# The first normalisation of a two-layer recurrent/attention network: its 128-row transposes made as pairs of 64-row transposes

## What is computed

```python
x = L0_attn_x                      # (4, 1024, 256)
xn = _layernorm(x, axis=-1)
s = _L0_attn_ref(xn, ...)          # begins with h = _layernorm(xn, ln_g, ln_b), then Q, K, V = h @ W.T
g = _silu(_L0_ffn_ref(xn, ...))    # begins with logits = xn @ gate_w.T (16 experts)
x = x + s * g
xn = _layernorm(x, axis=-1)
s = _L1_attn_ref(xn, ...)          # 16 heads of 64, causal softmax
g = _silu(_L1_ffn_ref(xn, ...))    # 8 experts, top 2
x = x + s * g
```

## Time and profile before

| | us |
|---|---|
| Median of three runs | 2710.64 |
| The three runs | 2716.63, 2710.22, 2710.64 |
| The profiled execution | 2716.68 |
| Its span | 2714.9 |
| First normalisation, first to last TensorE work | 19.14 to 64.49 |
| First TensorE work of the next stage | 67.65 |

### The profile page before, as it was taken

How to read it: one execution, slowest core, us unless ns; L and a number is a source line. 1 busy time by engine, 2 the same in 40 slices (tenths; PEclk the granted TensorE clock), 3 DMA queues, 4 the chain that set the end, 5 groups by cost and what they waited for, 6 DMA issues and landing times. The chain is left out here.

```text
span 2714.9 us, 45734 instructions
## 1 busy us (share of the span) xinstructions
PE 2490.7 (92%) x14584; PEld 1728.2 (64%) x14585; DVE 1288.0 (47%) x3160; ACT 1132.6 (42%) x2593; POOL 536.7 (20%) x485
## 2 busy tenths in 40 slices
PE   6999996999992689999999999999999998999993
PEld 6445553555551556666666666666666667999993
DVE  5454542211224546556566566565655653333334
ACT  3122121111112446666666666666666664222222
POOL 3000002444423133233111111111111110111113
PEclk8999998999995589999999999999999999999997
DMA  5001012876434333222211112111221124667796
GB/s 183 31 31 46 15 46 94 255 215 179 116 70 119 125 117 101 78 85 82 57 31 46 46 44 56 39 39 46 62 55 46 54 66 156 240 235 240 243 332 225
DMA packets 144829, 295.30 MB, mean 109 GB/s; under 512 B 16784, under 2 KB 102560, under 8 KB 134400
## 3 DMA queue, kind: packets, MB, share of 16 engines
q1 hardware_dynamic: 123824, 251.62, 29.0%
q0 software_dynamic: 20944, 42.94, 6.2%
HBM read 193.83 MB, written 67.12 MB: 96 GB/s over the span
## 5 line engine op out<-in xcount | busy, mean ns | idle before, releaser
L1364 DVE CUSTOM_DVE_ANT_0 at_p<-at_ps,atk_mask 128x640 f32<-128x640 f32 (+7 forms) x512 | 375.7, 753 | 262.7 <-PE at_ps L1228 147.9
L1282 ACT ACTIVATE at_pT<-at_ps 128x512 f32<-128x512 f32 (+1 forms) x640 | 327.1, 554 | 214.8 <-PE at_ps L1228 213.3
L1275 ACT ACTIVATE at_p<-at_p,at_nmax 128x640 f32<-128x640 f32 (+7 forms) x512 | 391.5, 768 | 58.1 <-DVE at_nmax L1364 55.8
L1307 POOL TENSOR_TENSOR at_qkT<-at_raw,at_swapped 128x1024 f32<-128x1024 f32 x64 | 150.8, 2356 | 1033.7 <-DVE at_swapped L1379 1033.7
L1228 PEld LDWEIGHTS at_ps<-atk_ident,at_p 128*128 128x128 f32 x2304 | 255.6, 141 | 142.6 <-issue 127.6
L1394 DVE SCALAR_TENSOR_TENSOR late_y<-at_ps,at_inv,late_y 128x256 f32<-128x256 f32 x512 | 215.1, 477 | 224.5 <-PE at_ps L1249 205.8
L1228 PE MATMUL at_ps<-atk_ident,at_p 128*128 128x128 f32 x2304 | 316.1, 278 | 5.3 <-ACT at_pT L1282 3.3
L1218 PE MATMUL at_ps<-at_qkT 64*128 64x512 f32 (+3 forms) x1536 | 292.5, 499 | 6.9 <-POOL at_qkT L1307 3.8
L1239 PE MATMUL at_ps<-at_pT,at_v 128*64 128x256 f32 (+1 forms) x2560 | 277.2, 363 | 0.0
L1200 PE MATMUL at_ps<-atk_h,atk_w 128*128 128x512 f32 x512 | 242.7, 597 | 15.5 <-SPq L1074 15.5
L1239 PEld LDWEIGHTS at_ps<-at_pT,at_v 128*64 128x64 f32 x2560 | 172.2, 136 | 99.4 <-issue 21.2
(11 more groups left out here) (214 smaller groups left out, 3300.0 us busy)
## 6 DMA issues: line engine op xcount, KB each, us to landing
moe_w<-in_w_w SPq DMA_DIRECT2D x53, 1028.0 KB, 4.5
at_swapped<-at_raw SPq DMA_DIRECT2D x256, 128.0 KB
late_w<-in_w_w SPq DMA_DIRECT2D x18, 1028.0 KB, 4.4
atk_w<-in_w_qkv SPq DMA_DIRECT2D x32, 384.0 KB
slot_in<-ex_zero SPq DMA_DIRECT2D x9, 1032.0 KB
xn_n<-n_stage SPq DMA_DIRECT2D x8, 1024.0 KB, 4.6
ex_wg<-in_w_eg SPq DMA_DIRECT2D x16, 512.0 KB
ex_wu<-in_w_eu SPq DMA_DIRECT2D x16, 512.0 KB
```

The lines of the kernel that those rows point to most:

```text
L1275: act.activation(buf, buf, ACT.Exp, bias=nmax[:, unit:unit + 1], scale=-1.0, accum_out=rsum[:, unit:unit + 1]).then_inc(exp_done, 1)
L1282: act.activation(dst, ring[RING_BANK[part][ev]][:, 0:(i1 - i0) * P].rearrange("p (k c) -> p k c", c=P), ACT.Copy).then_inc(t_read, 1)
L1307: pool.tensor_tensor(out=qkT[x][:, :].rearrange("p (m t) -> p m t", m=2)[:, :, half * CH:(half + 1) * CH], in0=raw[half][:, :].rearrange(" ...
L1364: dve.tensor_tensor_reduce(out=p[unit % LAG][:, 0:(n[0] + 1) * P], in0=scores(*n), in1=mask[:, T - (n[0] + 1) * P:T], scale=-1.0, scalar=3 ...
```

## The change

Only the call with `first` true is changed. Each 128 x 128 transpose becomes two: the upper 64 rows of the block and the lower 64 rows of it, each with the 64 x 64 corner of the identity as moving data. The two are issued one behind the other, in different row halves of TensorE, and they write 64 columns each to two different banks. Three pairs of banks (0 and 1, 2 and 3, 4 and 5) are used in turn by the half batches of `turn_stage` and `turn_scaled`. A half batch now fills a pair of banks with both halves of the channels (`c`), so ScalarE's evictions of a half batch both wait until its 16 half transposes are done. An eviction reads 256 columns of each of the two banks and puts them in order in `xnT` or `hT`. TensorE waits, before a half batch, for the evictions of the half batch three before it, in a common order of `stage` and `scaled`. The logits and the order of the three steps of a batch stay as they were.

```diff
+        def half_pair(b, kind, half):
+
+            at = (4 * b + 2 * kind + half) % 3 * 2 * CH
+            return s.all_banks[:, at:at + 2 * CH].rearrange("p (r c i x) -> p c r i x", r=2, c=KC, x=DH)
...
+                def turn_halves(b, kind, src, signal):
+
+                    for half in range(2):
+                        event = 4 * b + 2 * kind + half - 3
+                        if event >= 0:
+                            pe.wait_ge((stage_read, scaled_read)[event % 4 // 2], 4 * (event // 4) + 2 * (event % 2) + 2 + ONE)
+                        for c in range(KC):
+                            for i in range(4):
+                                at = (half * 4 + i) * C + c * P
+                                for r in range(2):
+                                    rows = slice(r * DH, (r + 1) * DH)
+                                    last = pe.transpose(half_pair(b, kind, half)[:, c, r, i, :], src[rows, at:at + P], ident[rows, rows])
+                            last.then_inc(signal, 1)
+
                 def turn_stage(b):
+                    if first:
+                        return turn_halves(b, 0, stage[b % 2], stage_ps)
...
                 def turn_scaled(b):
                     pe.wait_ge(scaled_made, b + 1 + ONE)
+                    if first:
+                        return turn_halves(b, 1, scaled[b % 2], scaled_ps)
...
                 def stage_evicted(b, j):
                     half, c = j // 2, j % 2
-                    act.wait_ge(stage_ps, 4 * b + j + 1 + ONE)
+                    act.wait_ge(stage_ps, 4 * b + (2 * half + 1 if first else j) + 1 + ONE)
...
-                    act.activation(dst, ps[j], ACT.Copy).then_inc(stage_read, 1)
+                    src = ps[j]
+                    if first:
+                        dst, src = dst.rearrange("p (i r x) -> p r i x", r=2, x=DH), half_pair(b, 0, half)[:, c]
+                    act.activation(dst, src, ACT.Copy).then_inc(stage_read, 1)
...
                 def scaled_evicted(b, j):
                     half, c = j // 2, j % 2
-                    act.wait_ge(scaled_ps, 4 * b + j + 1 + ONE)
+                    act.wait_ge(scaled_ps, 4 * b + (2 * half + 1 if first else j) + 1 + ONE)
...
+                    src = ps[4 + (4 * b + j) % 3]
+                    if first:
+                        dst, src = dst.rearrange("p (i r x) -> p r i x", r=2, x=DH), half_pair(b, 1, half)[:, c]
+                    act.activation(dst, src, ACT.Identity, scale=gain[:, c:c + 1], bias=off[:, c:c + 1]).then_inc(scaled_read, 1)
```

More of the change, by code:

```diff
@@ L474, in scaled_evicted @@
                         dst = (d.at_h if b == 0 else tall[b % 2])[:, c * T + half * CH:c * T + (half + 1) * CH]
-                    act.activation(dst, ps[4 + (4 * b + j) % 3], ACT.Identity, scale=gain[:, c:c + 1], bias=off[:, c:c + 1]).then_inc(scaled_read, 1)
+                    src = ps[4 + (4 * b + j) % 3]
+                    if first:
+                        dst, src = dst.rearrange("p (i r x) -> p r i x", r=2, x=DH), half_pair(b, 1, half)[:, c]
+                    act.activation(dst, src, ACT.Identity, scale=gain[:, c:c + 1], bias=off[:, c:c + 1]).then_inc(scaled_read, 1)
                 if not first:
```

## The result

The changed kernel takes 2716.36 us (median of 20 runs, 2711.08 to 2719.59) against 2711.33 us (20 runs, 2707.13 to 2716.78). The ratio is 1.0017, with a 95% interval of 1.0011 to 1.0024: 3.0 to 6.5 us slower. The forecast was 2723 us, +12.5 us, with a range of 2711 to 2732 us. The sign was right and the reason only in part. The size was not right: the 5 us measured are two fifths of the forecast, and less than the 8 us that I had set as the bound of "slower".

The account below looks back on a forecast made before the run. The prediction took TensorE, busy for 92% of the span, to bound the kernel. Clock 9.8, waits 0.7 and 0.8, and row changes 1.2 made +12.5 us on the median 2710.64: 2723 us, range 2711 to 2732.

Parts of the forecast that it names:

- the bound of "slower": Whole kernel: 0.3%, 8 us, about what a measurement can tell from no change; slower by more had chance 0.68.
- I book 0 for the pace: Transposes: a pair of halves costs one load of 128 columns, 0.214 us at 1.2 GHz, as before; 0 us.
- The lower bound that I had given for a pair: Transposes: if the matmul's columns alone counted, a pair takes 0.107 us and the 128 transposes save 13.7 us.
- The clock, +9.8 us: Changed stage: half-full transposes do not raise the clock, so it stays at 1.2 GHz throughout; 54.9 us instead of 45.1.
- 0.50 from the first transposes to the barrier: Expected sign in the profile after: granted clock at 0.50 (1.2 GHz) through the whole stage.
- The waits, +0.7 and +0.8 us: ScalarE's evictions: first logits begin 0.7 us later, the stage's end comes 0.8 us later; 0 in later batches.
- The stall that I had named for the high clock: Later batches: at the high clock 8 transposes no longer cover the evictions, about 0.6 us a batch.
- Changing between halves and full rows, +1.2 us: Between transposes and logits: 8 changes between row halves and full rows, 0.15 us each at the low clock.
- The base: Whole kernel: the sum was added to the median, 2710.64 us, not to the profiled execution, 2716.68 us.
- Rival 1: Changed stage: the clock goes on as before, leaving waits, changes and stalls; about +3 us, 2714 us; chance 0.23.
- Rival 2: Transposes: the two loads of a pair run one after the other; +40 us, 2751 us; chance 0.04.
- Rival 3: Transposes: a pair is quicker than one full load and the clock goes on as before; -8 us, 2702 us; chance 0.05.

Follow-up runs that it names:

- same_half: Changed kernel with both transposes of a pair reading the upper 64 rows, lower rows left out: 2727.21 us in a single execution (kernel before: 2711.47).
- half_logits: Changed kernel with each logits matmul made as two of 64 rows, into banks 6 and 7, which VectorE adds: ratio 1.0013 to the kernel before.
- second profile: Kernel before, unchanged, profiled again in a later execution: 2709.94 us, where the first profile has 2716.68 us.
- late_signals: Kernel before, with ScalarE told of both channel halves together, after 8 full transposes instead of 4: 2707.68 against 2704.49 us.
- warm_before: Kernel before, with 30 matmuls that serve only the clock ahead of its first transpose: 2708.23 against 2711.47 us.
- wide_logits: Changed kernel with each logits matmul streaming its 16 gate columns up to eight times over: ratio 1.0003 to the kernel before.
- vector_evicts: Changed kernel with VectorE evicting the second half of each batch and ScalarE the first: ratio 1.0017 to the kernel before.
- unpaired: Changed kernel with four half transposes of the upper rows, then four of the lower: 2718.58 us in a single execution (kernel before: 2710.27).
- best: Changed kernel, logits streaming up to 128 columns, clock-only matmuls (30 before the first transpose, 5 ahead of each batch's logits): 2705.74 against 2711.47 us for the kernel before.
- best_full: As best, but with full transposes of 128 rows in place of the halves: 2699.06 against 2703.36 us for the kernel before.
- filled: As wide_logits, plus clock-only matmuls, 50 before the first transpose and 10 ahead of each batch's logits: 2711.73 against 2710.27 us for the kernel before.

## Why the prediction was wrong in its size

- **"So a pair costs one load of 128 columns, as before: 0.214 us ... I book 0 for the pace."** This step failed. A pair takes 0.11 us. The logits showed a load of 0.214 us, and I gave the transposes the same one. But half logits kept 0.2 us a pair and half transposes did not. Nor does the load hold a full transpose (L556 keeps the pace with half of it): its matmul does, which the prediction named as possible in one parenthesis and then dropped. That it is the matmul's columns and not its rows is the plainest reading, but not shown. The lower bound that I had given for a pair, 0.107 us, was its true price; the 13.7 us that go with it were not saved, since logits and waits grew. The loads of the earlier trace rows are those of ordinary fp32 matmuls; they said nothing of a transpose.
- **The clock, +9.8 us.** That the change would lose the gift of the clock was right, and the ground for it was wrong. With pairs at 0.11 us a run of transposes streams as densely as before; it is its length that is halved, with a wait behind it. The forecast "0.50 from the first transposes to the barrier" was wrong: the clock rose twice in the profile after, each time too late for more than a part of the logits. Measured against the first profile the logits lost 24.3 - 19.3 = 5.0 us, against the second 8.8 us. `same_half` has the stage that I forecast, with transposes that use one row half at a time.
- **The waits, +0.7 and +0.8 us.** The first logits start 3.6 us behind the first transpose as before: the shorter transposes and the longer wait cancel. In the later batches, where I had booked 0, the wait is 1.2 us each, since the cover, 1.7 us of transposes per half batch, was gone with the first step. The stall that I had named for the high clock came at the low one. At the end ScalarE is 64.57 - 62.60 = 2.0 us behind TensorE instead of 0.8: +1.2 us.
- **Changing between halves and full rows, +1.2 us.** Logits to transposes take 6.94 us where they took 6.85, so 0.1 us a batch; in `half_logits`, where both are halves, it is 6.85 again. The other change is inside the wait. The drain that the Trainium skill names is there, and small.
- **The base.** Profile and median were 6 us apart, and I added the sum to the median. The sum was reckoned against a profile that had little of the clock's gift. The second profile shows most of the 6 us to lie in this stage, as the prediction had left open.
- **The rivals.** Rival 1 (the clock goes on as before) was wrong in its mechanism, but its 2714 us lay nearer to the time. Rival 2 is excluded at 0.11 us a pair. Rival 3 was half right: the pair is cheaper by 0.1 us, far over its 0.02 us; but the clock did not go on as before, and that took back more than the pair gave.

The Trainium skill says in "TensorE: Matmul & The Clock Gate", Part 4, that transposes do not count as busy. The profiles with full fp32 transposes speak against it (both of before, `late_signals` and `warm_before`): once TensorE is at work in the stage, every rise comes in or right behind a run of them, as at 45.66 us in the first profile. Part 3 of the same page of the Trainium skill gives tiles in different row groups as concurrent; `same_half` agrees, with 3.46 us against 1.76 for 32 halves.

What stays open: how the 5 us divide between the waits and the clock. `late_signals` has 3.2 us (0.8 to 6) without a half transpose, `wide_logits` gets about 4 us back without touching the waits, and `vector_evicts` gets nothing back without most of them; so the two are not independent. Half transposes with the early signals of before, which would price the halves alone without fills, were not run.

## What to carry to other kernels

Price a new operation by rows of the same kind: a load under a transpose and a load under a matmul had the same length in the trace only because something else set one of them. When a stage runs at a changing clock, a change that makes one part faster can cost more than it gives: here the three groups of `scaled` transposes between batches took 5 us less, and the logits and waits took more than that back. Look at what the clock does for the neighbours first, and at more than one execution. Wide logits and a few matmuls in the waits took 4 to 6 us off the kernel before, and with them the whole kernel no longer showed how the transposes were made.

## What the hardware did that I had not expected

- A full fp32 transpose of 128 x 128 takes 0.214 us at 1.2 GHz; two of 64 x 128 with 64 columns take 0.11 us in the two row halves together, and 0.216 us in one. With four of one row half ahead of four of the other, TensorE still started them in twos, 0.013 us apart (`unpaired`). At 2.4 GHz, 16 blocks take 1.05 us in halves and 1.75 us in full, both in the profiles with the clock held (`best`, `best_full`).
- A matmul of the code is two in the trace (16 calls of the logits are 32), a transpose is one. The text ahead of the prediction counts the trace's.
- Streaming 128 columns instead of 16 under the same load costs nothing (3.76 us a batch at the high clock in `best` against 3.75 in the second profile of before). With the fills beside them the clock stayed at 1.00 through such logits in `best` and `filled`; through the logits of 16 columns it fell in `warm_before`, which began as warm.
- Four evictions out of two banks, 64 columns at a time, take 2.79 us back to back with gain and offset, as they do from one bank (2.78 in `best_full`).
